# Involution block: which taps GpSimd takes and when, and how the row maxima are laid out

## The reference, cut to what matters

```python
N, CIN, H, Wd = (4, 256, 56, 56); REL, OUT, SHARE = (32, 256, 8); K, PAD = 7, 3; LOC = 32
x1 = conv1x1(x, w1, b1); x2 = conv1x1(x, w2, b2); x3 = conv1x1(x, w3, b3)
p = conv1x1(position(h, w, x.dtype), wp, bp)
sub2 = x1[:, :, None] - unfold_patches(x2)          # 49 taps (i, j)
subp = p[:, :, None] - unfold_patches(p)
feat = concatenate([sub2, subp], axis=1).reshape(n, REL + 2, K * K, h * w)
y = relu(bn_eval(feat, bn1...)); y = conv1x1(y, cw1)
y = relu(bn_eval(y, bn2...)); wgt = conv1x1(y, cw2, cb2)
wgt = softmax(wgt, axis=2).reshape(n, LOC, K * K, h, w)   # over the 49 taps
x3p = pad(x3, reflect)
for i in range(K):
    for j in range(K):
        out = out + x3p[..., i:i+h, j:j+w].reshape(n, LOC, SHARE, h, w) * wgt[:, :, i*K+j][:, :, None]
```

## Time and profile before

| | |
|---|---|
| median of 3 runs | 3883.24 us (3878.19 to 3886.63) |
| profiled execution | 3877.12 us, span 3875.3 us, mean TensorE clock 0.918 |
| `conv_stage` in it | 175 to 1718 us |
| busy over the whole span | PE 81%, DVE 66%, ACT 52%, POOL 51% |
| one slot (774.5 to 881.5 us), 107.0 us | PE 84.1, DVE 99.6, ACT 64.9, POOL 94.9 us busy |

### The profile page before, as it was taken

The page is one execution under the profiler, slowest core; times in us unless marked ns, Lnnn a source line. Parts: engine busy times, 40 slices in busy tenths (PEclk is TensorE's granted clock), DMA queues, the critical chain, the costliest instruction groups (busy, mean ns, idle before and its releaser), DMA issues. The chain is left out here.

```text
span 3875.3 us, 102116 instructions
## 1 busy us (share of the span) xinstructions
PE 3125.9 (81%) x42750; PEld 1556.8 (40%) x42750; DVE 2569.3 (66%) x2229; ACT 2013.4 (52%) x3476; POOL 1962.9 (51%) x1032
## 2 busy tenths in 40 slices
PE   4767777878787777757989999999999994588797
PEld 1224444434343444324343524353344432355465
DVE  6259999999999999977456735664565545444212
ACT  1275556666666555524756575557556653334120
POOL 1269888988899898854140504051223401422422
PEclk9888899999999888888999999999999997788898
DMA  5611111111111111120121102111111103333443
GB/s 202 196 56 56 47 57 49 43 59 59 57 57 55 55 55 47 31 70 26 26 60 48 46 11 58 58 26 26 53 48 26 26 20 100 127 122 124 126 128 117
DMA packets 169451, 257.40 MB, mean 66 GB/s; under 512 B 81600, under 2 KB 128616, under 8 KB 165944
## 3 DMA queue, kind: packets, MB, share of 16 engines
q1 hardware_dynamic: 157120, 219.82, 18.8%
q0 software_dynamic: 11392, 31.02, 2.5%
q10 hardware_dynamic: 504, 0.05, 0.0%
HBM read 152.29 MB, written 79.27 MB: 60 GB/s over the span
## 5 line engine op out<-in xcount | busy, mean ns | idle before, releaser
L742 PE MATMUL ps<-prod,ident 32*32 32x504 f32 x17472 | 935.8, 646 | 257.2 <-issue 180.5
L679 DVE TENSOR_TENSOR prod<-ps,win 128x3584 f32<-128x3584 f32 x280 | 1054.5, 3790 | 99.7 <-PE ps L742 56.1
L1065 POOL TENSOR_TENSOR phk<-kv 128x768 f32<-128x768 f32 (+1 forms) x200 | 349.2, 1751 | 964.6 <-ACT kv L1173 902.6
L742 PEld LDWEIGHTS ps<-prod,ident 32*32 32x32 f32 x17472 | 380.5, 108 | 464.5 <-issue 413.9
L1217 ACT ACTIVATE phq<-ps 128x896 f32<-128x896 f32 x448 | 384.3, 917 | 212.7 <-PE ps L1501 211.8
L457 POOL TENSOR_TENSOR y<-a1w,x2w 128x1568 f32<-128x1568 f32 x98 | 345.9, 3538 | 137.5 <-PE ps L723 120.4
L466 POOL TENSOR_TENSOR ex<-lg,mx 128x1568 f32<-128x1568 f32 x98 | 345.1, 3541 | 16.0 <-DVE mx L665 15.8
L1501 PE MATMUL ps<-qst,sel 96*128 96x448 bf16 x1120 | 293.0, 365 | 25.1 <-ACT phq L1217 7.0
L561 ACT ACTIVATE ps<-ex 128x448 f32<-128x448 f32 x280 | 148.4, 533 | 293.9 <-DVE prod L679 293.9
L1316 DVE TENSOR_TENSOR phk<-ps,kv 128x1280 f32<-128x1280 f32 (+1 forms) x200 | 295.4, 1480 | 0.7 <-ACT ps L1177 0.7
L483 POOL TENSOR_TENSOR osb<-ex,win 128x1792 f32<-128x1792 f32 x70 | 270.2, 3859 | 28.5 <-PE ps L742 28.5
(11 more groups left out here) (261 smaller groups left out, 5283.7 us busy)
## 6 DMA issues: line engine op xcount, KB each, us to landing
win<-planes SPq DMA_DIRECT2D x14, 2480.0 KB, 9.0
pf<-pf_dram SPq DMA_DIRECT2D x392, 55.1 KB
qst<-qsp SPq DMA_DIRECT2D x96, 196.0 KB, 4.7
planes<-stage SPq DMA_DIRECT2D x7, 1984.0 KB, 7.0
xs<-in_x SPq DMA_DIRECT2D x8, 1568.0 KB, 21.4
conv_dram<-osb SPq DMA_DIRECT2D x56, 224.0 KB, 4.8
t<-in_x SPq DMA_DIRECT2D x28, 448.0 KB, 4.0
xn<-conv_dram SPq DMA_DIRECT2D x28, 448.0 KB, 6.3
```

The source lines that it names most:

```text
L679: v.tensor_tensor(o, w, xw, ALU.mult).then_inc(prod_ready, 1)
L742: mm = pe.matmul(ps[32 * h:32 * h + 32, 4 + r, 0:DENC], diag(ident, r), x[32 * r:32 * r + 32, h].rearrange("p s w -> p (s w)"), start=begi ...
L1065: pool.tensor_tensor(phk[j % 2][0:r, :, ROT_V * DH:FLIN].rearrange("p h (r i) -> p h r i", i=DH), ki.unsqueeze(2).broadcast_to([r, HPG, RO ...
```

## The change

GpSimd's ten own taps are taps 7 to 16 (all of tap row 1 and three of row 2) in place of 39 to 48, and their steps are spread: 3, 5, 7, 9, 11, 13, 14, 15, 16, 18. The pairs take the other 39 taps, so pairs 0 to 2 and the first half of pair 3 are row 0 and the second half of pair 3 is tap 17 of row 2. The ninth plane of an own tap is written by ScalarE (`own_denominators`), one step before the tap is added. The logits lie pixel by pixel with the seven taps of a row next to each other; a row maximum is a reduction of seven neighbours (L669), and one reduction (L675) over the seven rows' maxima replaces the folds. TensorE's first matmul reads `y1` and GpSimd's `shift` reads `lg` with steps for this. Relu i is at step 2i, and the exponentials of rows 2 to 6 at steps 0, 2, 5, 8, 11; row 1's comes after the first weights. The accumulation now ends with the last pair, so `acc_done` is gone. What GpSimd waits for before it overwrites `ex` is counted by row.

```diff
 OWN = 10
+OWN_TAPS = list(range(K7, K7 + OWN))
+PAIR_TAPS = [t for t in range(TAPS) if t not in OWN_TAPS]
...
-EXP_NOW = {FOLD_AT + 1: 0, FOLD_AT + 2: 1}
-EXP_NEXT = {2: 2, 4: 3, 6: 4, 8: 5, 10: 6}
-FIRST_AT = [0] + [2 * i - 1 for i in range(1, K7)]
...
-OWN_AT = [NPAIR_D - OWN + k for k in range(OWN)]
+EXP_FIRST_AT = FOLD_AT + 1
+EXP_NEXT = {0: 2, 2: 3, 5: 4, 8: 5, 11: 6}
+FIRST_AT = [2 * i for i in range(K7)]
...
+OWN_AT = [3, 5, 7, 9, 11, 13, 14, 15, 16, 18]
...
-        lg = sb("lg", [P, K7, RW, K7, W])
+        lg = sb("lg", [P, K7, PW, K7])
...
-        run = sb("run", [P, RW, K7, W])
+        run = sb("run", [P, PW, K7])
...
             def shift(b, i):
                 pool.wait_ge(maxed, b.n + 1)
                 if not b.early(1):
-                    pool.wait_ge(den_in, NPAIR_D * (b.n - 1) + FREE_ROW_PAIRS if i < FREE_ROW else NPAIR_D * b.n)
-                if i == FREE_ROW and not b.early(1):
-                    pool.wait_ge(own_ready, 2 * OWN * b.n)
+                    if pairs_of_row(i):
+                        pool.wait_ge(den_in, NPAIR_D * (b.n - 1) + pairs_of_row(i))
+                    if own_to_row(i):
+                        pool.wait_ge(own_den, OWN * (b.n - 1) + own_to_row(i))
+                        pool.wait_ge(own_ready, OWN * (b.n - 1) + own_to_row(i))
+                l = lg[:, i].rearrange("p (h w) j -> p h j w", w=W)
...
-                pool.tensor_tensor(ex[:, i], lg[:, i], m, ALU.subtract).then_inc(shifted, 1)
+                pool.tensor_tensor(ex[:, i], l, m, ALU.subtract).then_inc(shifted, 1)
...
                 if k == 1 and not b.early(1):
                     pool.wait_ge(stored, 16 * RW * b.n)
-                if k >= 2:
-                    pool.wait_ge(own_used, (OWN - 1) * b.n + k - 1)
+                if k >= 2 or not b.early(1):
+                    pool.wait_ge(own_used, OWN * b.n + k - 1)
...
-                pool.tensor_copy(o[:, :, SHARE], w).then_inc(own_ready, 1)
...
                 if a:
                     shift(a, 0)
-                    shift(a, 1)
                 if b:
                     own(b, OWN - 1)
+                if a:
+                    shift(a, 1)
...
+            def own_denominators(b, k):
+                i, j = OWN_TAPS[k] // K7, OWN_TAPS[k] % K7
+                act.wait_ge(exped, b.q(i) + 1)
+                if k == 1 and not b.early(1):
+                    act.wait_ge(stored, 16 * RW * b.n)
+                if k >= 2 or not b.early(1):
+                    act.wait_ge(own_used, OWN * b.n + k - 1)
+                act.activation(own_buf[k % 2][:, :, SHARE], ex[:, i, :, j, :], ACT.Copy).then_inc(own_den, 1)
...
                     if a and u in FIRST_AT:
                         first(FIRST_AT.index(u))
+                    if b and u + 1 in OWN_AT:
+                        own_denominators(b, OWN_AT.index(u + 1))
                 if a:
                     weights(a, 0)
                     weights(a, 1)
                     denominators(a, 0)
+                    expo(a, 1)
...
-                    v.tensor_tensor(run[:], lg[:, i], lg[:, 0] if i == 1 else run[:], ALU.max).then_inc(ranmax, 1)
+                    v.tensor_reduce(run[:, :, i], lg[:, i], AX.X, ALU.max).then_inc(ranmax, 1)
...
-                    v.tensor_tensor(mx[:].rearrange("p (h w) -> p h w", w=W), run[:, :, 0], run[:, :, 1], ALU.max).then_inc(maxed, 1)
+                    v.tensor_reduce(mx[:], run[:], AX.X, ALU.max).then_inc(maxed, 1)
...
-                            pe.matmul(ps[at:at + 32, k + r // 2, 0:CW].rearrange("p (j w) -> p j w", w=W), diag(cw1, r),
-                                      y[32 * r:32 * r + 32, :, h * W:(h + 1) * W], start=True, stop=False)
+                            pe.matmul(ps[at:at + 32, k + r // 2, 0:CW].rearrange("p (w j) -> p w j", j=K7), diag(cw1, r),
+                                      y[32 * r:32 * r + 32, :, h * W:(h + 1) * W].rearrange("p j w -> p w j"), start=True, stop=False)
```

More of the change, by code:

```diff
@@ L223, in _ @@
             v.wait_ge(pstep, 3)
-            v.tensor_tensor(ud[:], pq[:, 0, :], pq[:, 1, :], ALU.subtract).then_inc(pstep, 1)
+            by_pixel = [pq[:, k, :].rearrange("p (j w) -> p w j", w=W) for k in range(2)]
+            v.tensor_tensor(ud[:].rearrange("p (w j) -> p w j", j=K7), by_pixel[0], by_pixel[1], ALU.subtract).then_inc(pstep, 1)
             v.tensor_scalar(vd[:], hq[:, 1:1 + K7], hq[:, 0:1], -1.0, ALU.subtract, ALU.mult).then_inc(pstep, 1)
@@ L333, with pairs_of_row, own_to_row @@
 FOLD_AT = MAX_AT[-1]
-EXP_NOW = {FOLD_AT + 1: 0, FOLD_AT + 2: 1}
-EXP_NEXT = {2: 2, 4: 3, 6: 4, 8: 5, 10: 6}
-FIRST_AT = [0] + [2 * i - 1 for i in range(1, K7)]
-POOL_ORDER = [("z", 0), ("z", 1), ("shift", 2), ("shift", 3), ("z", 2), ("shift", 4), ("shift", 5), ("z", 3), ("shift", 6),
-              ("z", 4), ("z", 5), ("own", 0), ("own", 1), ("z", 6)] + [("own", k) for k in range(2, OWN - 1)]
-OWN_AT = [NPAIR_D - OWN + k for k in range(OWN)]
+EXP_FIRST_AT = FOLD_AT + 1
+EXP_NEXT = {0: 2, 2: 3, 5: 4, 8: 5, 11: 6}
+FIRST_AT = [2 * i for i in range(K7)]
+POOL_ORDER = [("z", 0), ("z", 1), ("shift", 2), ("shift", 3), ("own", 0), ("z", 2), ("own", 1), ("shift", 4), ("z", 3), ("own", 2),
+              ("shift", 5), ("z", 4), ("own", 3), ("shift", 6), ("own", 4), ("z", 5), ("own", 5), ("z", 6), ("own", 6), ("own", 7),
+              ("own", 8)]
+OWN_AT = [3, 5, 7, 9, 11, 13, 14, 15, 16, 18]
 SCALE_AT = 1
-NMAX = K7 + 1
+def pairs_of_row(i):
+    return max([p // 2 + 1 for p, t in enumerate(PAIR_TAPS) if t // K7 == i], default=0)
+def own_to_row(i):
+    return sum(t // K7 <= i for t in OWN_TAPS)
 class Blk:
@@ L473, in own @@
                 pool.wait_ge(exped, b.q(i) + 1)
-                if k == 0 and not b.early(1):
-                    pool.wait_ge(acc_done, b.n)
                 if k == 1 and not b.early(1):
                     pool.wait_ge(stored, 16 * RW * b.n)
-                if k >= 2:
-                    pool.wait_ge(own_used, (OWN - 1) * b.n + k - 1)
+                if k >= 2 or not b.early(1):
+                    pool.wait_ge(own_used, OWN * b.n + k - 1)
                 w = ex[:, i, :, j, :]
@@ L517, in load_win @@
                 if not a.early(2):
-                    sp.wait_ge(acc_done, a.n - 1)
+                    sp.wait_ge(summed, NPAIR_D * (a.n - 1))
                 sp.dma_start(win[a.par][:], planes[:, bass.ds(a.n * RW, RW + K7 - 1)]).then_inc(win_in[a.par], 16)
@@ L551, in tap_pair @@
                 n = min(2, ND - 2 * p)
-                at = [t // K7 * K7 * PW + t % K7 * W for t in range(2 * p, 2 * p + n)]
+                at = [t // K7 * K7 * PW + t % K7 * W for t in PAIR_TAPS[2 * p:2 * p + n]]
                 e = ex[:]
@@ L636, in divide @@
                 acc = ps[:, 4:8]
-                v.wait_ge(acc_done, m + 1)
+                v.wait_ge(summed, NPAIR_D * (m + 1))
                 v.reciprocal(den, acc[:, :, SHARE * W:DENC]).then_inc(divided, 1)
@@ L674, in pair @@
                     w = ps[:, 2 + p % 2, 0:n * PW].rearrange("p (n h w) -> p n h w", h=RW, w=W).unsqueeze(3).broadcast_to([P, n, RW, SHARE, W])
-                    at = [t // K7 * SHARE * WP + t % K7 for t in range(2 * p, 2 * p + n)]
+                    at = [t // K7 * SHARE * WP + t % K7 for t in PAIR_TAPS[2 * p:2 * p + n]]
                     x = win[b.par][:]
```

51 lines of the change are left out of this document (17 added, 34 removed).

## The result

The changed kernel took **4189.61 us** (median of 4 runs, 4182.02 to 4195.02), the kernel before 3883.23: a ratio of 1.0784 (95% interval 1.0767 to 1.0802), slower. The profiled execution took 4191.27 us, its span is 4189.5 us, 314.2 more than before. The forecast of 4110 had the sign and lay 80 us low; its range held the time, its own narrower range (4050 to 4190) only just.

A forecast was written before the change was run, and what follows sets the result against it. VectorE bounds the kernel, with the TensorE-ScalarE chain close behind. Five marks sum to +16.1 us per slot, +18.1 with TensorE's step, 217 over twelve; 225 in all on 3877.1 is 4102, so 4110, range 3990 to 4280.

The forecast's parts named there:

- TensorE's step: First matmul of a group reading y at 896-byte steps: +0.3 us per group taken, 2 us a slot.
- Mark 1: Pair 0 to the first L718: Exp of row 2 now ahead of the awaited Relu, 16.3 us, +5.4.
- Mark 3: Fourth L718's end to the seventh: own tap 1 and ScalarE wait for the osb store, 25.3 us, +13.0.
- rings: Chain groups alternating TensorE and ScalarE, the next L718 waiting for L592: 4.3 us each, 5.05 with an own tap.
- Mark 4: Seventh to fourteenth L718: 38.5 us of chain work plus 2.6 waiting for GpSimd's z 5, 41.1, +2.3.
- Mark 5: Fourteenth L718 to the next pair 0: cheaper maximum, one fold for three, less waiting for weights, -6.5 us.
- mark 2: First L718 to the fourth's end: Exp of row 3 and Relu of row 1 between groups, 17.5 us, +1.9.
- The start: Outside the twelve slots: 2 us more at the start, some 7 in the slot without a store wait.
- Steps are free: Rival: shift stays at 3.5 us and L718 as before, 86 us less, 4020; chance 0.15.
- steps cost as in the stage copies: Rival: GpSimd's shift takes 6.9 us, 14 us more per slot, 4280; chance 0.12.
- the store does not bind: Rival: store lands before own tap 1 is due, fourth to seventh L718 adds 1 us, near 3950; chance 0.09.
- VectorE stays the bound: Rival: the slot is VectorE's work, 91 us plus 6 idle, 97, ten less, 3750 us; chance 0.07.

The follow-up runs named there:

- early_store: Changed kernel with SyncE storing the divided block ahead of the position features of row 2 instead of behind those of row 3; 4073 us, ratio 1.0496.
- layout_only: Kernel before with only the new layout of the logits and the maxima as TensorReduces, taps, steps and waits as before; ratio 1.0073, slot 108.3 us.
- z_after: Changed kernel with GpSimd writing z pixel by pixel, so that TensorE reads y without steps; ratio 1.0544, slot 123.9 us.
- store_relu: Changed kernel with two order edits, the store ahead of the features of row 2 and the Relu one step earlier; ratio 1.0085, slot 109.1 us.
- z_after_sr: Changed kernel with z written pixel by pixel (TensorE without steps), the store ahead of row 2's features and the Relu one step earlier; ratio 0.9968.
- schedule_only: Changed kernel with its taps, steps and waits, but logits, two-source maxima, folds, subtraction and first matmul laid out as before; ratio 1.0552.
- z_before: Kernel before with the new layout but z written pixel by pixel, TensorE without steps, old taps and tables; ratio 0.9796, slot 100.7 us.

## Why the prediction was right, and where it was short

By its own five marks (a slot from pair 0 at 763.50 to pair 0 at 893.61, 130.1 us; L728 groups 1, 4, 7, 14 at 779.20, 798.14 with its end near 800.4, 826.93, 870.52):

| mark | before | forecast | after |
|---|---|---|---|
| 1 pair 0 to first L728 | 10.9 | 16.3 | 15.7 |
| 2 to the end of the fourth | 15.6 | 17.5 | 21.2 |
| 3 to the seventh | 12.3 | 25.3 | 26.5 |
| 4 to the fourteenth | 38.8 | 41.1 | 43.6 |
| 5 to the next pair 0 | 29.3 | 22.8 | 23.1 |
| sum | 106.9 | 123.0 | 130.1 |

(The forecast column leaves out the 2 us for TensorE's step, which it put at no mark.)

- **Mark 1** right, by its cause: Exp of row 2 waits 7.6 us for shift 2 at 776.05, the Relu stands behind it, and L728 starts at 779.20.
- **Mark 3, the new wait,** right: osb waits 22.5 us per slot (269.5 in twelve), L584 7.1 (85.7 in twelve); the forecast said 15 or more, and some 6. The stores are issued at 804.16, 3.8 after the fourth group's end (forecast 3.6), and have landed 8.6 after that (forecast 7.6); from there to the seventh L728 it is 14.2 (forecast 14.1). early_store shows it to be a cause: without it the slot is 9.2 shorter. The forecast said 12 for that case, and 3950. Without the wait the three groups from the fourth L728 to the seventh take 19.0 us (769.00 to 788.04), 5.6 more than before (800.00 to 813.40), where the forecast had 1 more: 3.2 of it are two Relus from row to row, the rest the longer rings. That is why one edit alone gives 116 us and not 160.
- **Mark 4** came out near its number, but not by its working. The forecast took 38.5 for the rings with Relus, Exp and own taps, and 2.6 more because ScalarE would ask for z 5 before GpSimd had it. GpSimd needed what was said (37.3 us to the end of z 5, forecast 38.1), yet no Relu waited for it, and ScalarE waited for TensorE alone from 827 to 871 us:

```profile
846.78 3.32 POOL L464 TENSOR_TENSOR y<-a1w,x2w 128x1568 f32<-128x1568 f32 x1
...
850.62 0.91 ACT L608 ACTIVATE lg<-ps,par 128x784 f32<-128x784 f32 x1 [0.20 <-PE ps L744]
851.43 1.50 ACT L590 ACTIVATE y<-y 128x1568 f32<-128x1568 f32 x1
```

  The Relu starts behind L608, 1.3 us after z 5 is done, and of all 98 Relus of the run one found ScalarE idle for z (24.0 us at the start of the stage):

```profile
L590 ACT ACTIVATE y<-y x98: 1493/1500/1511, 184.7 to 1911.2; 128x1568 f32<-128x1568 f32 x98
...
  POOL y L464: 24.0, 1
```

  early_store agrees: there GpSimd is not held by the store, and mark 4 is 44.3 (788.04 to 832.33), no shorter than the 43.6 here. What fills the mark is the chain: 38.5 and seven groups at 0.68 more are 43.3. The 2.6 that did not come hid as much of TensorE's step; that was luck.
- **Mark 5** right: one fold of 1.79 us, and the wait for weights gone.
- **The term that was mis-sized is TensorE's step.** "I take +0.3, which over the groups that lie on the path gives 2 us a slot." The bounds were nothing and +0.66 per group; layout_only has +0.68, the upper bound. The groups on the path were counted well (2 / 0.3 is about seven; the 5 to 7 us of z_after are seven to ten at 0.68, the 3.6 between store_relu and z_after_sr five). It sits in marks 2 and 4, where 3.7 and 2.5 us were missing (5.1 without the 2.6 for GpSimd): from the first to the fourth L728 z_after is 1.7 us shorter, from the seventh to the fourteenth 4.1. By the 5 to 7 us of z_after, 3 to 5 of the 6 us by which 18.1 fell short of 24.1 are the step. Some 2 us of mark 2 stay open; TensorE was granted only 0.60 of its clock from 779 to 783 us and 0.64 from 793 to 797, and what that costs there was not taken apart. I had taken the middle of the bounds, although the argument for the upper one stood beside it: VectorE's stepped L1330, whose rate I had used in full for GpSimd.
- **The start** was a second miss: 22.6 us up to the first of the divisions counted, against 9 forecast for the start and the slot without a store wait. The runs point at the first slots' chain, and not at the store: the same division comes at 375.3 us after the change, 372.1 in early_store, 361.3 with the Relu early, 358.8 in z_after, 355.1 in schedule_only, 364.4 in layout_only and 352.6 before. Each is one execution. Taking back the late Relu removes 14.0 of the 22.6, taking back TensorE's step 16.5 (with the faster z), so the two overlap and together cover it; how they share it stays open. With 72 from the slots and about 4 from the later stages it makes up the 89 between 4102 and 4191.
- **Shift**: 4.33 against 4.5 taken, within its bounds: 0.79 us more where 1.0 was taken. By the Trainium skill's cycle (GPSIMD Engine Reference, "Performance pitfalls for Q7 kernels") it would have been 4.8, an estimate; the trace has 0.79 us for 1568 elements, 0.6 of that cycle.
- **TensorReduce**: 1.78 against 1.7. By the Trainium skill (SBUF — State Buffer, "Who interferes with whom") it never contends with GpSimd; the trace agrees: 1.776 to 1.789 us in 98 instructions, while GpSimd was busy for 5 to 8 tenths of the stage's slices.
- **The ten copies on ScalarE** at nothing: 0.38 us each, and except where L584 waits for the store nothing waits on them.
- **The rivals.** "Steps are free" falls by the shift at 4.33 and L728 at 835 ns, "steps cost as in the stage copies" by the shift too (6.9 said), "the store does not bind" by early_store. "VectorE stays the bound" is the case of z_before: slot 100.7 where the rival said 97, but there with the old taps, so that no store and no Relu stand in the ring. The point from which I let it decide (two rings with a Relu below two pairs and a maximum) is met there: 8.8 (768.43 to 777.30, 777.30 to 786.13) against 9.3, the Relu being hidden.

## What to carry to other kernels

Before work is spread to shorten a bound, follow every buffer that it uses to its last reader: here the second own tap, which moved from step 11 of the slot to step 5, writes a buffer whose store is queued behind other transfers, and held up the queues of two engines. A step in an access pattern cost something on each of the four engines that took it here; give it to the engine that can write the data in another order at no price (here GpSimd's z), or to one that is idle, and not to an instruction in a ring. And where two waits lie in series in one period, removing one shows little: test them together as well as apart. And where a forecast comes out near, check each of its terms against the trace: here a wait that never came covered for part of a cost taken too low.

## What the runs showed of the hardware

- A stepped operand cost on every engine, for fp32: TensorE 835 against 488 ns for 392 columns, read at 896 bytes (0.89 ns per column); VectorE 3.14 against 1.78 us for 1568, read at 224 bytes (0.87 ns per element); ScalarE 1.70 against 0.91 us for 784, written at 28 bytes (1.0 ns); GpSimd 4.33 against 3.54 us for 1568, one of two sources read at 28 bytes (0.5 ns).
- An instruction of 835 in place of 488 ns lengthened the pass of sixteen on four row groups by 0.68 us, twice the difference of one.
- The stepped matmul did not follow the clock: 815 to 902 ns in all 3136 (the unstepped one 484 to 858), and the first nine of a group took 1.49 us both at 779.20, where 0.60 of the clock was granted (779 to 783 us), and at 784.59, where it was 1.00.
- GpSimd's z with an innermost run of 7, overlapping reads and one broadcast source was faster than with runs of 56: 3.00 against 3.27 us.
